# Two fp32r dense layers, second-layer buffers dealt out in another order, and identities added in the first layer

## The reference, cut to what matters

```python
def _cxin_conv(x, a, eps, W, b):
    ax = a @ x
    h = ax + (1.0 + eps[0]) * ax
    for i in range(3):
        h = jax.nn.relu(h @ W[i].T + b[i])
    return h
# x: 4096x128, adj: 4096x4096, all float32
out1 = _cxin_conv(x,  adj, eps1, W1, b1)
out2 = _cxin_conv(x2, adj, eps2, W2, b2)
x = layernorm(x + jnp.concatenate((out1, out2), axis=1) @ Wm.T + bm)
A_hat = adj + jnp.eye(4096)
d = where(rowsum(A_hat) > 0, rsqrt(rowsum(A_hat)), 0)
y = (d[:, None] * A_hat * d[None, :]) @ x
x = layernorm(x + y @ W.T + b)
```

## Time and profile before

| | us |
|---|---|
| median of 3 runs | 594.17 |
| lowest and highest | 594.01, 595.21 |
| the profiled execution, device time | 593.58 |
| its span in the profile | 591.8 |
| PE busy | 584.8 (99%) |
| DVE busy | 540.5 (91%) |
| ACT busy | 372.2 (63%) |

### The profile page before, as it was taken

The page is one execution under the profiler, slowest core; times in us unless marked ns, Lnnn a source line. Parts: engine busy times, 40 slices in busy tenths (PEclk is TensorE's granted clock), DMA queues, the critical chain, the costliest instruction groups (busy, mean ns, idle before and its releaser), DMA issues.

```text
span 591.8 us, 7721 instructions
## 1 busy us (share of the span) xinstructions
PE 584.8 (99%) x2676; PEld 484.3 (82%) x2676; DVE 540.5 (91%) x679; ACT 372.2 (63%) x494; POOL 28.7 (5%) x31
## 2 busy tenths in 40 slices
PE   8999999999999999999999999999999999999996
PEld 7888888888888888888888888867888888888885
DVE  6999999997988998998799999994899999989986
ACT  6554446842544773454667336486897888898893
POOL 1000000001100000110000020000200010010011
PEclk9999999999999999999999999999999999999998
DMA  9978565443554533354443375776699999999911
GB/s 334 370 271 296 202 226 197 142 148 137 214 205 170 190 145 142 142 213 174 181 150 138 138 293 189 286 299 212 245 353 413 364 370 383 400 365 374 387 42 71
DMA packets 27849, 141.56 MB, mean 239 GB/s; under 512 B 2608, under 2 KB 3376, under 8 KB 13616
## 3 DMA queue, kind: packets, MB, share of 16 engines
q1 hardware_dynamic: 27248, 139.54, 63.6%
q10 hardware_dynamic: 576, 1.70, 0.7%
HBM read 139.14 MB, written 2.10 MB: 239 GB/s over the span
## 4 chain that ended last, share of the span: by engine, by line
PE 98%; issue 0%; DVE 0%; POOL 0%; POOLq 0%; DVEq 0%
PE ps L468 81%; PE ps L544 7%; PE pd L486 6%; PE pd L497 2%; PE pd L530 1%; PE pd L592 1%; POOLq L118 0%; POOL rstd L1119 0%; DVE z L1090 0%; PE pd L494 0%; DVE stats L1095 0%; DVE outn L1104 0%; POOL identity L1123 0%; DVE mv L897 0%; DVEq L118 0%
## 5 line engine op out<-in xcount | busy, mean ns | idle before, releaser
L649 ACT ACTIVATE ahi<-raw 128x1024 fp32r<-128x1024 f32 x212 | 221.7, 1057 | 165.4 <-PE ps L468 152.8
L816 DVE TENSOR_TENSOR alo<-raw,ahi 128x1024 fp32r<-128x1024 f32 x212 | 257.2, 1220 | 29.7 <-ACT ahi L649 27.9
L468 PE MATMUL ps<-ahi,x2s 128*128 128x512 f32 x512 | 138.4, 389 | 0.0
L468 PE MATMUL ps<-ahi,x1hi 128*128 128x512 f32 x384 | 121.8, 393 | 0.0
L468 PE MATMUL ps<-alo,x1hi 128*128 128x512 f32 x384 | 120.5, 390 | 0.0
L468 PE MATMUL ps<-ahi,x1lo 128*128 128x512 f32 x384 | 120.4, 389 | 0.0
L468 PEld LDWEIGHTS ps<-ahi,x2s 128*128 128x128 f32 x512 | 96.1, 188 | 20.0
L468 PEld LDWEIGHTS ps<-ahi,x1hi 128*128 128x128 f32 x384 | 71.9, 188 | 15.9 <-issue 1.4
L468 PEld LDWEIGHTS ps<-alo,x1hi 128*128 128x128 f32 x384 | 72.0, 188 | 15.2 <-DVE alo L816 0.3
L468 PEld LDWEIGHTS ps<-ahi,x1lo 128*128 128x128 f32 x384 | 72.1, 188 | 14.9
L468 PE MATMUL ps<-alo,x2s 128*128 128x512 f32 x256 | 80.3, 389 | 0.0
(11 more groups left out here) (98 smaller groups left out, 510.7 us busy)
## 6 DMA issues: line engine op xcount, KB each, us to landing
raw<-a_t SPq DMA_DIRECT2D x108, 1024.0 KB, 4.9
raw<-a_t SPq DMA_DIRECT2D x32, 512.0 KB, 7.4
raw<-early SPq DMA_DIRECT2D x7, 512.0 KB, 7.8
xn<-x SPq DMA_DIRECT2D x3, 1024.0 KB, 8.1
out<-outn ACTq DMA_DIRECT2D x3, 512.0 KB, 6.7
par<-params SPq DMA_DIRECT2D x1, 708.0 KB, 12.8
raw<-head SPq DMA_DIRECT2D x2, 256.0 KB, 3.2
xn<-x SPq DMA_DIRECT2D x1, 512.0 KB, 7.2
```

Source lines behind the costliest of these rows:

```text
L468: mm = pe.matmul(ps[bank + (CH * (q % 2) if layer else 0)][:, :], block_of(w, n), a[c], start=(n == 0 and k == 0), stop=(n == JB - 1 and k ...
L649: act.activation(ring_hi(layer, q, n), raw_tile(layer, n), ACT.Copy).then_inc(hi_ready, 1)
L816: dve.tensor_tensor(ring_lo(layer, q, n), raw_tile(layer, n), as_f32(ring_hi(layer, q, n)), ALU.subtract).then_inc(lo_ready, 1)
```

## The change

It does four things, all around the border between the two layers.

1. **Dense layers.** In the last MLP (`plan` 1) the second and third dense layers become fp32r with three products, like those of the other quarters. ACT writes each relu twice from the same PSUM block, once as `h` and once rounded as `hhi`, and DVE subtracts the two into `h_rest`, which lies in the memory of `h`. The first dense layer stays float32.
2. **Places.** `PE_DENSE[1]` goes from tiles 1, 2, 3 to 1, 3, 5, the merge from 4 to 6, the relus of ACT from 7, 8, 9 to 4, 6, 7. The residual stays after tile 10. The transpose of the row sums goes from tile 4 to 2 and the reduction from 5 to 2. `y` is made after tile 17, rounded after 18 and split after 19.
3. **Buffers.** Slots 4 and 5 of the rounded tiles get memory of their own, `ahi_extra`; the first of these lies where `rowsum_all` was, and so ACT waits for the transpose before tile 5. The eight pair buffers of layer two are used in the order 4, 5, 0, 1, 6, 2, 3, 7 (`SLOT1`) where they were used from 0 to 7.
4. **Identities.** All eight of the first quarter are added in layer one, after its tiles 24 to 31.

```diff
-PE_DENSE = ({3: 0, 5: 1, 8: 2}, {1: 0, 2: 1, 3: 2})
-PE_MERGE = (10, 4)
+PE_DENSE = ({3: 0, 5: 1, 8: 2}, {1: 0, 3: 1, 5: 2})
+PE_MERGE = (10, 6)
+DVE_SPLIT_H = {4: 1, 6: 2}
...
-ACT_RELU = tuple({k + ahead: l for k, l in plan.items()} for plan, ahead in zip(PE_DENSE, AHEAD_OF_PE))
-DVE_RESIDUAL = tuple(k + ahead for k, ahead in zip(PE_MERGE, AHEAD_OF_PE))
+ACT_RELU = ({k + SPLIT: l for k, l in PE_DENSE[0].items()}, {4: 0, 6: 1, 7: 2})
+DVE_RESIDUAL = (PE_MERGE[0] + SPLIT, PE_MERGE[1] + SPLIT)
...
-DVE_TURN = (5, 4)
+DVE_TURN = (5, 2)
...
-DVE_MAKE_Y = (KB + 4, 2 * KB + 4, 3 * KB + 3, 18)
+DVE_MAKE_Y = (KB + 4, 2 * KB + 4, 3 * KB + 3, 17)
...
+SLOT1 = (4, 5, 0, 1, 6, 2, 3, 7)
...
+        with ExitStack() as until_turned:
+            rowsum_all = until_turned.enter_context(nc.sbuf_tensor("rowsum_all", [P, QW], F32))
+        ahi_extra = [sb(f"ahi_extra{i}", [P, QW], F32R) for i in range(SPLIT2 - SPLIT)]
+        with ExitStack() as whole:
+            h = whole.enter_context(nc.sbuf_tensor("h", [P, M, CW], F32))
+        h_rest = sb("h_rest", [P, M, CW], F32R)
...
-            p %= RAW + RAW2
+            p = SLOT1[p % (RAW + RAW2)]
...
-            if i >= SPLIT:
-                m = 2 * (i - SPLIT)
-                return hhi[:, m:m + 2, :].rearrange("p m w -> p (m w)")
-            return ahi[:, i, :]
+            return ahi[:, i, :] if i < SPLIT else ahi_extra[SPLIT2 - 1 - i][:, :]
...
+                    elif l:
+                        wait(pe, hlo_ready, q * (LAYERS * M) + (M * (l - 1) + m + 1))
+                        passes = ((whi, hhi), (whi, h_rest), (wlo, hhi))
...
+                if layer == 1 and q == 0 and n == SPLIT2 - 1:
+                    act.wait_ge(turned_ready, QUARTERS)
...
+                    if plan == 1 and l < LAYERS - 1:
+                        act.activation(hhi[:, m, :], pd[:, m, :], ACT.Relu,
+                                       bias=par[:, at:at + 1]).then_inc(hhi_ready, 1)
...
+                if plan == 1:
+                    wait(dve, h_ready, q * (4 * M) + (M * l + m + 1))
+                wait(dve, hhi_ready, q * (LAYERS * M) + (M * (l - plan) + m + 1))
+                dve.tensor_tensor((hlo, h_rest)[plan][:, m, :], h[:, m, :], as_f32(hhi[:, m, :]),
                                   ALU.subtract).then_inc(hlo_ready, 1)
...
-                        if n + AHEAD >= JB:
-                            add_identity(0, n + AHEAD - JB)
+                        if n >= JB - KB:
+                            add_identity(0, n + KB - JB)
...
-                        if n + AHEAD < KB:
-                            add_identity(q, n + AHEAD)
+                        if n in DVE_SPLIT_H:
+                            for m in range(M):
+                                split_h(LAST, DVE_SPLIT_H[n], m, 1)
```

More of the change, by code:

```diff
@@ L142, in build @@
         raw = sb("raw", [P, RAW, 2, QW])
+        with ExitStack() as until_turned:
[4 more added lines that the diff above has]
+        h_rest = sb("h_rest", [P, M, CW], F32R)
         ahi = sb("ahi", [P, SPLIT, QW], F32R)
         alo = sb("alo", [P, SPLIT, QW], F32R)
-        h = sb("h", [P, M, CW])
         hhi = sb("hhi", [P, M, CW], F32R)
-        rowsum_all = sb("rowsum_all", [P, QW])
         partial = sb("partial", [P, QW // TB])
@@ L267, in raw_tile @@
                 return raw[:, p % RAW, n % 2, :]
-            p %= RAW + RAW2
+            p = SLOT1[p % (RAW + RAW2)]
             return raw[:, p, n % 2, :] if p < RAW else raw2[:, p - RAW, n % 2, :]
         def wait_raw1(eng, q, n):
-            s, turn = n // 2 % (RAW + RAW2), n // 2 // (RAW + RAW2)
+            s, turn = SLOT1[n // 2 % (RAW + RAW2)], n // 2 // (RAW + RAW2)
             per_quarter = 16 * PAIRS // (RAW + RAW2)
@@ L380, in load2 @@
                 sp.wait_ge(block_used, (QUARTERS - 1) * JB + (g + 1) * KB)
-                load(raw2[:, g], RAW + g).then_inc(raw2_in[g], 16)
+                load(raw2[:, g], SLOT1.index(RAW + g)).then_inc(raw2_in[g], 16)
             groups = QUARTERS * PAIRS // RAW
@@ L398, in _ @@
                 sp.wait_ge(raw_used, groups * RAW + s + 1 - RAW)
-                load(raw[:, s], s).then_inc(raw_in[s], 16)
-                if s == 0:
+                load(raw[:, s], SLOT1.index(s)).then_inc(raw_in[s], 16)
+                if s == 1:
                     load2(2)
@@ L404, in _ @@
             with sp.Fori(1, turns - turns // QUARTERS) as g:
-                for s in range(RAW + RAW2):
-                    sp.wait_ge(lo_ready, g * (2 * (RAW + RAW2)) + (QUARTERS * JB + 2 * (s + 1 - RAW - RAW2)))
+                for i, s in enumerate(SLOT1):
+                    sp.wait_ge(lo_ready, g * (2 * (RAW + RAW2)) + (QUARTERS * JB + 2 * (i + 1 - RAW - RAW2)))
                     dst, landed = (raw[:, s], raw_in[s]) if s < RAW else (raw2[:, s - RAW], raw2_in[s - RAW])
-                    load(dst, g * (RAW + RAW2) + s).then_inc(landed, 16)
+                    load(dst, g * (RAW + RAW2) + i).then_inc(landed, 16)
             for m in range(PAIRS):
-                s, c = m % (RAW + RAW2), m // (PAIRS // CH)
+                i, c = m % (RAW + RAW2), m // (PAIRS // CH)
+                s = SLOT1[i]
                 pair = LAST * PAIRS + 2 * QUADS[c][m % (PAIRS // CH)]
@@ L415, in _ @@
                 dst, landed = (raw[:, s], raw_in[s]) if s < RAW else (raw2[:, s - RAW], raw2_in[s - RAW])
-                for r, done in enumerate((unit_in[s], landed)):
+                for r, done in enumerate((unit_in[i], landed)):
                     sp.dma_start(dst[:, r, :].rearrange("p (t w) -> p t w", w=CW),
@@ L831, in sum_rows, with split_h @@
                     dve.tensor_tensor(to[:, :], rowsum[:, :], tile, ALU.add).then_inc(raw_used, 1)
-            def split_h(q, l, m):
-                wait(dve, hhi_ready, q * (LAYERS * M) + (M * l + m + 1))
-                dve.tensor_tensor(hlo[:, m, :], h[:, m, :], as_f32(hhi[:, m, :]),
+            def split_h(q, l, m, plan):
+                if plan == 1:
+                    wait(dve, h_ready, q * (4 * M) + (M * l + m + 1))
+                wait(dve, hhi_ready, q * (LAYERS * M) + (M * (l - plan) + m + 1))
+                dve.tensor_tensor((hlo, h_rest)[plan][:, m, :], h[:, m, :], as_f32(hhi[:, m, :]),
                                   ALU.subtract).then_inc(hlo_ready, 1)
@@ L915, in mlp_step @@
                         for m in range(CH):
[L916 to L919, removed]
+                            split_h(q, 0, CH * (n - ACT_EVACUATE[0] - 1) + m, 0)
+                if plan == 0 and n in ACT_RELU[0] and ACT_RELU[0][n] < LAYERS - 1:
+                    for m in range(M):
+                        split_h(q, ACT_RELU[0][n] + 1, m, 0)
                 if n == DVE_TURN[plan]:
                     turn_rowsums(q)
-                if n == DVE_TURN[plan] + 1:
+                if n == DVE_TURN[plan] + 1 - plan:
                     add_turned(q)
```

## The result

The changed kernel takes 595.78 us (median of 22 runs, 595.11 to 597.6), the kernel before 594.56 us on the same chip (22 runs, 593.83 to 596.65): a ratio of 1.002, interval 1.0014 to 1.0026, so 1.22 us more. The forecast was 1.0 us more. Of the 0.58 us between 595.2 and 595.78, 0.39 us is the kernel before, which stood at 594.17 in three runs and at 594.56 in 22. The profiled execution took 595.71 us with a span of 593.8, against 593.58 and 591.8.

The account below looks back on a forecast made before the run. PE, busy without a break, was taken to bound the kernel. -1.45 us in the dense layers plus waits of 0.70, 0.49, 0.35 and 0.91 gave +1.0 on 594.17: 595.2 us, own range 594.6 to 595.7, wide range 593.4 to 596.1.

Parts of the forecast that it names:

- The dense layers: Second and third dense layers of the last MLP: 2.75 us each as fp32r, 1.45 us less on PE.
- 20 writes on ACT, 0.575 us apart: ACT's relu writes between rounding tiles 4 and 8: spacing read from the trace; 0.61 us apart would add 0.8 us.
- `z` held by ACT, at 412.63: Residual after tile 10: DVE, tied to ACT after tile 6, can start it at 412.63, against a merge done at 412.48.
- `dall` at 420.80, tile 13's rest at 422.14, `yt` at 426.56, tile 20's rest at 433.41: Layer two's first quarter, after the residual: clock times in us at which DVE's steps were to come.
- Tile 13 waits 0.70: Layer two's first quarter: PE wants tile 13's rest at 421.44, DVE has it at 422.14, a 0.70 us wait.
- Tiles 19 and 20 wait 0.49 + 0.35 + 0.91 = 1.75: Around `y`: PE waits 0.49 us for ACT's rounding of tile 19, then 0.35 and 0.91 for DVE's splits of 19 and 20.
- The sum: At tile 20's rest: -1.45 + 0.70 + 0.49 + 0.35 + 0.91 = +1.0 us, PE running free from tile 21.
- PE's list of waits: Sign of being right: it names DVE `alo` about three times, 2 us together, and ACT's rounding near 429, 0.5 us.
- the gain stays: Rival, after the merge: waits over 2 us smaller than found, so the dense layers' gain remains, 592.7 us; chance 0.08.
- Half of it: Rival: only tile 13's wait is real, `y` hidden by PE's small delays, -0.75 us, 593.5 us; chance 0.12.
- Slow ACT pairs: Rival, ACT's relu writes: pairs cost 1.25 us, not 1.15, 8 pairs 0.8 us later, +1.8 us, 595.9 us; chance 0.24.
- Identities: Rival, layer one: identities wait for a pair not landed and hold DVE, 0.5 us on top, 595.7 us; chance 0.06.

Follow-up runs that it names:

- e10: Changed kernel with ACT normalising from tile 15, `dall` after tile 14, `y` made after 18, rounded after 20, split after 22: 592.93 us, ratio 0.9974.
- e6: Changed kernel with two more 128x512 ACT copies into `z` between tile 7's rounding and the third relu: 596.50 us, ratio 1.0032.
- e7: Changed kernel with two more 128x512 DVE additions into `yt` after tile 7's split: 595.50 us, ratio 1.0017.
- e3: Changed kernel with DVE's factor `dall` taken after tile 13 instead of tile 12: 594.96 us, ratio 1.0008.
- e4: Changed kernel with `y` rounded by ACT after tile 19 (not 18) and split by DVE after tile 20 (not 19): 594.89 us, ratio 1.0004.
- e2: Changed kernel with pair buffers in the old order, and first loads and identities as before: 595.92 us, ratio 1.0021.
- e5: Changed kernel with `dall` taken after tile 13, `y` rounded after tile 19 and split after tile 21: 593.51 us, ratio 0.9985.
- e9: The kernel before, unchanged, run once more for a second profile: 594.68 us, ratio 1.0001.

## Why the prediction was right, point by point

The positions are compared after taking 0.80 us off the trace of the changed kernel, since its last MLP starts that much later (393.51 against 392.71).

- *The dense layers*: 1.45 us less on PE. Right but for 0.06: 2.75 us each in e10's chain, where nothing hides it, and e10 is 1.51 us ahead.
- *20 writes on ACT, 0.575 us apart*: right, 0.573 measured. The figure worked out from the Trainium skill (ScalarE: Activation LUTs, What ACT_TABLE_LOAD costs), 0.61 us, would have made the eight writes of the first relu 4.9 us; they take 4.58. The trace decides, and the estimate from the page's constants is 7% too high for this form.
- *`z` held by ACT, at 412.63*: 412.68 measured, and e6 and e7 show the engine: 1.02 us for two ACT copies, nothing for two DVE additions. That it is the splits behind ACT and not the merge is by 0.22 us (0.15 in the prediction).
- *`dall` at 420.80, tile 13's rest at 422.14, `yt` at 426.56, tile 20's rest at 433.41*: 420.85, 422.21, 426.61 and 433.46. All within 0.07 us, since each is a chain of durations read from the rows.
- *Tile 13 waits 0.70*: 0.84 by position. PE wanted it 0.07 us earlier than worked out and got it 0.07 later. e3 takes this stop away and gains 0.75.
- *Tiles 19 and 20 wait 0.49 + 0.35 + 0.91 = 1.75*: 0.68 + 0.91 = 1.59 by position. PE was already 0.21 us later than in the sum (tile 18's third product at 429.15, by the sum 422.14 + 5 x 1.36 = 428.94), because of tile 13, so it waited less; the end of the stop is set by DVE, and that was right. e4 takes both away, has 0.43 at tiles 21 and 22 for them, and gains 1.22.
- *The sum*: +1.05 us at tile 20 against +1.0. But +1.19 at tile 24. **This is the term that was missing**: PE does not go on at full pace after a stop. The tile after each stop is 0.13 to 0.14 us late (424.50 - 423.01 = 1.49; 435.76 - 434.26 = 1.50). The one after tile 13 is taken up by the next stop, the one after tile 20 stays. What is won and lost up to tile 24 stays so to the end: from the dense start to the end of the span it is 200.28 us, against 199.08 before, +1.20. (The device times without their starts differ by 1.33; the 0.13 beyond lies outside the profile's span.)
- *Buffers and identities at nothing*: right, e2.
- *PE's list of waits*: half right. The stops are where they were said to be, but the list has two of them, 1.3 us, and ACT's stands only in PEld's timeline (0.58 us at 430.72, 429.92 on the clock of before). The sign asked the wrong view for a time that positions show in full.

The rivals: *the gain stays* would have needed smaller waits; e10 shows that this time exists, but only with other places. *Half of it* fell, since the `y` chain's stops are there (e4). *Slow ACT pairs* fell on its mechanism: 0.57 us between `h` and `hhi` from the same PSUM block. In the pairs of layer one the second write reads the first, and it starts 0.71 us after it (302.89 and 303.60), when the first one's 0.67 us are over. The time of that rival, 595.9, is nearer to the measured 595.78 than the forecast's 595.2; as a difference from before it is not (+1.8 and +1.0 against +1.22). That says how little the time alone tells about a mechanism; the positions tell it. *Identities* fell with e2.

The forecast's own range ended at 595.7 and missed the median by 0.08 us; the wide one held it. The line between "same" and "slower" was drawn at 1.2 us, and the difference of the medians is 1.22. The chances, about 0.49 for the same and 0.41 for slower as the prediction adds them up, said as much: it was not to be told from the profile on which side it would fall. The reference of three runs was itself 0.4 us low, and their spread of 1.2 us (594.01 to 595.21) gave warning of that. Small errors of both signs partly cancel in the sum: the waits come to 2.43 us by position where 2.45 were forecast, the two slow tiles after the stops (0.13 + 0.14) were left out, and the gain in the dense layers is 1.51 and not 1.45.

## What to carry to other kernels

Where two engines feed a third one and the third gets faster, write down for each step the position at which it is wanted and that at which it is there, in a ruler that starts at a common event; a single late hand-over (`z`) is paid wherever a step that waits stands in front of one that is wanted. Then don't speed up the late one, but move the waiting step behind the work that is wanted first: e10 keeps `z` as late as it is and moves five entries of the order, and that is worth 1.20 + 1.51 = 2.7 us by the ruler. To see whether an idle gap belongs to the engine that has it, put more work in it (e7: free) and on its neighbour (e6: paid in full).

## What the runs showed of the hardware

- A matmul that waits for its own weights costs more than the idle time that PE shows (2.70 us by position, 1.3 in PE's list). In the changed kernel PE shows 0.67 us of idle time at tile 13. PEld's timeline has 1.10 us at the same place:

```profile
423.00 0.30 PEld L472 LDWEIGHTS ps<-alo,x1hi 128*128 128x128 f32 x2 [1.10 <-DVE alo L828]
```

  The pair of matmuls after the stop shows 0.73 us instead of 0.62 on PE, and the tile as a whole is 0.13 us longer. In e5 a stop of 0.4 us on PEld cost 0.24 us with no idle time on PE at all. A possible reason is that after the stop the first weights are loaded with no product to run beside; that was not tested and no run shows it. For reading a trace it means: look at PEld's waits too, and take positions, not idle times.
- The same program starts its steady part at different times. The last MLP's first dense layer began at 392.71 and 393.82 us in two profiles of the kernel before, and at 396.20 in that of e7. That execution took 598.27 us, while e7's median is 0.3 us under the changed kernel's, so it is this one execution that started late and not the kernel. Its change stands 400 us behind the start; its chain has the first transfer at its head:

```profile
1.67 5.32 DMA raw<-head
...
7.78 12.29 PE ps L473 x46
```

  and that of the kernel before has PE's own start, with the tiles from 5.23 us on:

```profile
5.23 14.80 PE ps L468 x64
```

  2.55 of the 3.49 us are there already. Clock times of two executions of one kernel differed by 1.11 us here, distances inside them by 0.02 us (e9).
- Two ACT writes from the same PSUM block into different places start 0.57 to 0.59 us apart, as writes from different blocks do (395.16 to 395.73).
